# The feed-forward block of a Perceiver layer, run two groups further behind the output projection

## The chip, the cores and the metric

The kernel runs on one core of a Trainium2 chip, in one launch. The time is the device time of the program in microseconds (us). A core has TensorE (PE: matmuls and transposes, which write to PSUM), VectorE (DVE), ScalarE (ACT), GpSimd (POOL) and SyncE (SP, which here issues the DMAs). Each engine works through its own instruction list in order and waits on semaphores for the others.

## The reference

One layer of three blocks, each with a residual: cross-attention of x (32 x 32 x 256) to a context (32 x 257 x 256), causal linear attention with random features over 16 heads, and a feed-forward block with quantised inputs and ternary weights. The change touches only the end of the second block and the third:

```python
x = x + (y @ Wo)                                   # end of the linear attention
a = layernorm(x)
s = 127 / clip(max|a| over the row, 1e-5);  aq = round(a * s) / s
h = gelu(aq @ quantise(w1).T)                      # 256 -> 1024
t = 127 / clip(max|h| over the row, 1e-5);  hq = round(h * t) / t
x = x + hq @ quantise(w2).T                        # 1024 -> 256
```

Rounding is done by adding and then subtracting ROUND = 12582912; the integers are exact in bf16. The scales are per row, so each row's absmax must be known before anything of it is rounded.

## The kernel before

The 1024 rows of x are 8 groups (NG) of 128 rows, one row per partition. The first two blocks take the trace up to about 233 us and are not touched. The last stage runs over the groups; the order on each engine is written out by hand in a loop over i, in which each step works on the group `i - k` with a k of its own. For a group g the steps are, in the order in which the data passes:

- `yTt` (PE, L1079) transposes the attention's output in eight 128x128 blocks into the banks b0 and b1; `yTc` copies them to yT, half on ACT (shown at L387, the line of the helper `copy`), half on DVE (L784).
- `project_out` (PE, L1101): 16 fp32 matmuls into b2. The trace shows each as x16.
- `x2` (DVE): residual add (L796), then the statistics (L573, L576) and epsilon (L578). `rstd` (POOL, L295) takes the power -0.5.
- `quant_a` (DVE): normalises into xn3 (L583), absmax (L813) and three small operations for the scales (L802 to L805). `round_a` (POOL, L367) multiplies and adds ROUND; `cast_a` (ACT, L508) subtracts it into bf16 `aq`.
- `aqTt` (PE, L1109) transposes aq into b3, `aqTc` (ACT, helper `copy`) copies it to `aqT`. There is one aqT, so aqTc(g) waits until layer1 of group g-1 has read it (`h_mm`).
- `layer1` (PE, L1120): four bf16 matmuls 128x512 into b45, in two halves. `gelu` (ACT, L522) takes each half to `hid[g % 2]`.
- `quant_h` (DVE): absmax over 1024 columns (L818), then the scales. `round_h` (POOL, L373) writes hid times scale plus ROUND to `hr`, `cast_h` (ACT, L529) subtracts it into bf16 `hq`. hr and hq exist once each.
- `hqTt` (PE, L1129): eight transposes into b6, `hqTc` (ACT, helper `copy`) copies them to hqT.
- `layer2` (PE, L1139): eight bf16 matmuls into b7; it waits until `final` of the group before has read b7 (`fin_r`).
- `final` (DVE, L827): scales b7 and adds the residual, into `fin[g % 2]`. SP stores it.

Before the change layer1 and aqTt are one group behind project_out, gelu and quant_h two, hqTt and layer2 three, final four. When project_out of the last group is through, PE has by its list done layer1 of groups 0 to 5 and layer2 of groups 0 to 3.

Of the kernel before, what the change touches and what calls it, by code (L numbers as in the profile page):

```python
# [18 lines left out]
BF16 = mybir.dt.bfloat16  # L19
ALU = mybir.AluOpType  # L20
# [3 lines left out]
P = 128  # L24
B, T, D = 32, 32, 256
L = 257
NG = B * T // P
BG = P // T
PT = 2 * T
DC = D // P  # L30
# [5 lines left out]
HALF = NG // 2  # L36
# [5 lines left out]
ROUND = 12582912.0  # L42
# [3 lines left out]
def build(nc, x, ctx, ctxT, xWq, bq, xWk, bk, xWvT, bv, aWq, aWk, aWv, aWo, Wf, w1T, w2T,  # L46
          ident_d, mask_d, seq_d, out):
    with ExitStack() as stack:
        def sem(name):
            return stack.enter_context(nc.semaphore(name))  # L50

        def bank(name, shape, dt=F32):
            return stack.enter_context(nc.psum_tensor(name, shape, dt))
# [19 lines left out]
        w1q = keep.take("w1q", [P, DC, HID], BF16)  # L73
# [19 lines left out]
        qsc = keep.take("qsc", [P, 8, NG])  # L93
# [55 lines left out]
        z3 = Region(work_at)  # L149
# [1 line left out]
        xn3 = z3.take("xn3", [P, D])  # L151
        xr3 = z3.take("xr3", [P, D])
        aq = z3.take("aq", [P, D], BF16)
        aqT = z3.take("aqT", [P, DC, P], BF16)
        hid = [z3.take(f"hid{i}", [P, HID]) for i in range(2)]
        hr = z3.take("hr", [P, HID])
        hq = z3.take("hq", [P, HID], BF16)
# [6 lines left out]
        b0, b1, b2, b3 = (bank(f"b{i}", [P, 512]) for i in range(4))  # L164
        b45 = bank("b45", [P, 2, 512])
# [6 lines left out]
        def qk_bank(h, c):  # L172
# [41 lines left out]
        a_scale, ar_r, aq_r, aqT_mm, aqT_cp = (sem(n) for n in ("a_scale", "ar_r", "aq_r", "aqT_mm", "aqT_cp"))  # L214
        h_mm, h_act, h_scale, hr_r, hq_r, hqT_mm, hqT_cp, f2_mm, fin_r = (
            sem(n) for n in ("h_mm", "h_act", "h_scale", "hr_r", "hq_r", "hqT_mm", "hqT_cp", "f2_mm", "fin_r"))
# [60 lines left out]
        def _(pool):  # L277
# [15 lines left out]
            def rstd(n, g):  # L293
                pool.wait_ge(ln_var[n], g + 1)
                nc.gpsimd.tensor_tensor(lnr[:, n, g:g + 1], lnv[:, n, g:g + 1], mh[:, 0:1],  # L295
                                        ALU.pow).then_inc(ln_rstd[n], 1)
# [65 lines left out]
            def round_a(g):  # L362

                pool.wait_ge(a_scale, g + 1)
                if g >= 1:
                    pool.wait_ge(aq_r, g)
                nc.gpsimd.tensor_scalar(xr3[:], xn3[:], qsc[:, 2, g:g + 1], ROUND, ALU.mult, ALU.add).then_inc(ar_r, 1)  # L367

            def round_h(g):
                pool.wait_ge(h_scale, g + 1)  # L370
                if g >= 1:
                    pool.wait_ge(hq_r, g)
                nc.gpsimd.tensor_scalar(hr[:], hid[g % 2][:], qsc[:, 6, g:g + 1], ROUND, ALU.mult,  # L373
                                        ALU.add).then_inc(hr_r, 1)

            for i in range(NG + 2):
                if 0 <= i - 2 < NG:
                    round_h(i - 2)
                if i < NG:
                    rstd(2, i)  # L380
                    round_a(i)


        @block.scalar
        def _(act):
            def copy(dst, src):
                return nc.scalar.activation(dst, src, ACT.Copy)  # L387
# [121 lines left out]

            def aqTc(g):  # L510
                act.wait_ge(aqT_mm, g + 1)
                if g >= 1:
                    act.wait_ge(h_mm, 2 * g)
                copy(aqT[:], b3[:].bitcast(BF16)[:, 0:D]).then_inc(aqT_cp, 1)

            def gelu(g):
                if g >= 2:
                    act.wait_ge(hr_r, g - 1)
                act.wait_ge(out_scale[0], g + 1)
                for c in range(2):  # L520
                    act.wait_ge(h_mm, 2 * g + c + 1)
                    nc.scalar.activation(hid[g % 2][:, 512 * c:512 * c + 512], b45[:, c, :], ACT.Gelu,  # L522
                                         scale=qsc[:, 3, g:g + 1]).then_inc(h_act, 1)

            def cast_h(g):
                act.wait_ge(hr_r, g + 1)
                if g >= 1:
                    act.wait_ge(hqT_mm, g)
                nc.scalar.activation(hq[:], hr[:], ACT.Copy, bias=-ROUND).then_inc(hq_r, 1)  # L529

            def hqTc(g):
                act.wait_ge(hqT_mm, g + 1)
                if g >= 1:
                    act.wait_ge(f2_mm, g)
                copy(hqT[:], b6.bitcast(BF16)).then_inc(hqT_cp, 1)

            yTc(0)
            act.wait_ge(s_mask, STEPS)
            for i in range(NG + 4):
                if 0 <= i - 2 < NG:  # L540
                    gelu(i - 2)
                if 0 <= i - 1 < NG:
                    cast_a(i - 1)
                    aqTc(i - 1)
                if 0 <= i - 3 < NG:
                    hqTc(i - 3)
                if i + 1 < NG:
                    yTc(i + 1)
                if 0 <= i - 2 < NG:
                    cast_h(i - 2)  # L550


        @block.vector
        def _(dve):
# [261 lines left out]
            def quant_h(g):  # L816
                dve.wait_ge(h_act, 2 * g + 2)
                link(nc.vector.tensor_reduce(qsc[:, 4, g:g + 1], hid[g % 2][:], AX.X, ALU.max,  # L818
                                             apply_absolute_value=True))
                scales(4, 1, g, h_scale)  # L820

            def final(g):
                dve.wait_ge(f2_mm, g + 1)
                dve.wait_ge(out_scale[1], g + 1)
                if g >= 2:
                    dve.wait_ge(stored[g % 2], 16 * (g // 2))
                nc.vector.scalar_tensor_tensor(out=fin[g % 2][:], in0=b7[:, 0:D], scalar=qsc[:, 7, g:g + 1],  # L827
                                               in1=res[:, g, :], op0=ALU.mult, op1=ALU.add).then_inc(fin_r, 1)

            for i in range(NG + 4):  # L830
                if 0 <= i - 4 < NG:
                    final(i - 4)
                if 0 <= i - 2 < NG:
                    quant_h(i - 2)
                if i < NG:
                    x2(i)
                if i + 1 < NG:
                    yTc(i + 1)
                if i < NG:
                    quant_a(i)  # L840
# [3 lines left out]
        def _(pe):  # L844
# [8 lines left out]
            for m in range(DC):  # L853
                for c in range(DC):
                    mm = pe.matmul(b4[:, m * D:(m + 1) * D], xwq[:, c, m * P:(m + 1) * P], xwk[:, c, :],  # L855
                                   start=(c == 0), stop=(c == DC - 1))
# [7 lines left out]
            for m in range(DC):  # L864
                for c in range(DC):
                    mm = pe.matmul(b5[:, 260 + 2 * m:262 + 2 * m], xwk[:, c, m * P:(m + 1) * P],
                                   bqk[:, 0, c:c + 1].broadcast_to([P, 2]), start=(c == 0), stop=(c == DC - 1))
# [244 lines left out]
            def layer1(g):  # L1112
                pe.wait_ge(aqT_cp, g + 1)
                if g == 0:
                    pe.wait_ge(w_quant, 4)
                for hh in range(2):
                    if g >= 1:
                        pe.wait_ge(h_act, 2 * g - 1 + hh)
                    for c in range(DC):
                        mm = pe.matmul(b45[:, hh, :], aqT[:, c, :], w1q[:, c, 512 * hh:512 * (hh + 1)],  # L1120
                                       start=(c == 0), stop=(c == DC - 1))
                    mm.then_inc(h_mm, 1)

            def hqTt(g):
                pe.wait_ge(hq_r, g + 1)
                if g >= 1:
                    pe.wait_ge(hqT_cp, g)
                for c in range(HC):
                    mm = pe.transpose(b6.bitcast(BF16)[:, c * P:(c + 1) * P], hq[:, c * P:(c + 1) * P], identb[:])  # L1129
                mm.then_inc(hqT_mm, 1)  # L1130

            def layer2(g):
                pe.wait_ge(hqT_cp, g + 1)
                if g == 0:
                    pe.wait_ge(w_quant, 8)
                if g >= 1:
                    pe.wait_ge(fin_r, g)
                for c in range(HC):
                    mm = pe.matmul(b7[:, 0:D], hqT[:, c, :], w2q[:, c, :], start=(c == 0), stop=(c == HC - 1))  # L1139
                mm.then_inc(f2_mm, 1)  # L1140

            pe.wait_ge(f_exp, 8 * PAIRS)
            for i in range(NG + 4):
                if i < NG:
                    project_out(i)
                if 0 <= i - 1 < NG:
                    aqTt(i - 1)
                if 0 <= i - 3 < NG:
                    hqTt(i - 3)
                if i + 1 < NG:  # L1150
                    yTt(i + 1)
                if 0 <= i - 1 < NG:
                    layer1(i - 1)
                if 0 <= i - 3 < NG:
                    layer2(i - 3)


# [30 lines left out]
```

## Time and profile before

| | us |
|---|---|
| runs of the kernel before | 304.04, 306.99, 348.58 (median 306.99) |
| profiled execution, its own time | 302.64 |
| its span, first to last instruction | 300.1 |
| first project_out starts | 233.07 |
| last `final` | starts 297.40, takes 0.48 |
| store behind the last `final`, to landing | 1.7 |
| busy in the whole span: PE, DVE, ACT, POOL | 262.3, 169.3, 140.0, 127.4 |
| mean granted clock of PE, share of the full clock | 0.962 |

Times in the rows count from the first instruction of the span. A row of the timeline merges instructions of one line that follow each other on one engine; its time runs from the start of the first to the end of the last. A bracket at its end says how long the engine had been idle before it and what released it. In the chain of waits each piece is the time that it adds to the chain, so it can be shorter than the instructions themselves. PEld are weight loads, which run beside the matmuls.

### The profile page before, as it was taken

How to read it: one execution, taken by the hardware profiler on the slowest of the kernel's cores; microseconds unless marked ns; L12 is line 12 of the kernel's file. 1: busy time of each engine (PE TensorE's matmuls, PEld its weight loads, DVE VectorE, ACT ScalarE, POOL GpSimd, SP SyncE). 2: the span in 40 equal slices, each digit the busy share in tenths (PEclk: the TensorE clock that was granted, in tenths of full speed). 3: DMA queues.
4: the chain of work that ended last, by engine and by line, in shares of the span. 5: the costliest groups of instructions: out<-in, count | busy, mean ns of one | idle time of the engine just before them, and what ended most of it. 6: DMA issues, size and time to landing. Idle time of an engine off the chain costs nothing.

```text
span 300.1 us, 6276 instructions
## 1 busy us (share of the span) xinstructions
PE 262.3 (87%) x2438; PEld 192.0 (64%) x2442; DVE 169.3 (56%) x440; ACT 140.0 (47%) x260; POOL 127.4 (42%) x124
## 2 busy tenths in 40 slices
PE   0867848899997979999999999999989899999753
PEld 0743425566665757777777777777768777888532
DVE  4664567665543254555555555555555558777740
ACT  1032404233333775555555555555543055666662
POOL 2150044111021254558585858585894024323320
PEclk9996859999999999999999999999999999999995
DMA  7999985475019201000001010100000000000011
GB/s 231 323 369 400 351 298 151 167 282 141 3 9 367 78 8 30 20 20 16 22 2 35 4 37 2 35 2 2 2 0 2 2 1 2 17 19 20 17 35 35
DMA packets 17487, 26.70 MB, mean 89 GB/s; under 512 B 1428, under 2 KB 10804, under 8 KB 17460
## 3 DMA queue, kind: packets, MB, share of 16 engines
q1 hardware_dynamic: 17460, 26.32, 25.9%
q8 instruction: 19, 0.31, 0.4%
q14 instruction: 8, 0.07, 0.1%
HBM read 25.27 MB, written 1.05 MB: 88 GB/s over the span
## 4 chain that ended last, share of the span: by engine, by line
PE 75%; DVE 8%; ACT 5%; issue 5%; POOL 2%; DMA 2%; SPq 1%; POOLq 0%; DVEq 0%; ACTq 0%
PE b L1023 15%; PE b L847 9%; PE b L1101 8%; PE b L849 7%; PE b L848 7%; PE b L1048 6%; PE b L1036 5%; PE b L903 3%; PE b L1079 2%; PE b L926 2%; DMA bqk<-in_bk 2%; PE b L1139 2%; PE b L1120 1%; PE b L923 1%; PE b L855 1%
## 5 line engine op out<-in xcount | busy, mean ns | idle before, releaser
L490 ACT ACTIVATE phi<-b 128x512 f32<-128x512 f32 x64 | 34.8, 595 | 42.2 <-PE b L1023 42.2
L336 POOL TENSOR_TENSOR sq_lo<-sq,sq_hi 128x512 fp32r<-128x512 f32 x32 | 40.8, 1286 | 30.9 <-ACT sq_hi L448 30.1
L707 DVE CAST x_hi<-b 128x512 fp32r<-128x512 f32 x32 | 22.1, 691 | 46.7 <-ACT sq_hi L448 46.7
L295 POOL TENSOR_TENSOR lnr<-lnv,mh 128x1 f32<-128x1 f32 x16 | 8.8, 550 | 77.0 <-DVE lnv L578 77.0
L1101 PE MATMUL b<-wo,yT 128*128 128x256 f32 x128 | 29.3, 382 | 1.5 <-ACT yT L387 1.2
L847 PE MATMUL b<-nT_lo,wp_hi 128*128 128x512 f32 x64 | 27.0, 421 | 0.8 <-DVE x_lo L709 0.8
L1101 PEld LDWEIGHTS b<-wo,yT 128*128 128x128 f32 x128 | 23.7, 190 | 5.7 <-ACT yT L387 1.4
L849 PE MATMUL b<-nT_hi,wp_hi 128*128 128x512 f32 x64 | 25.4, 396 | 0.0
L848 PE MATMUL b<-nT_hi,wp_lo 128*128 128x512 f32 x64 | 25.3, 395 | 0.0
L447 ACT ACTIVATE sq<-b 128x512 f32<-128x512 f32 x32 | 19.2, 599 | 12.3 <-PE b L849 12.3
L709 DVE TENSOR_TENSOR x_lo<-b,x_hi 128x512 fp32r<-128x512 f32 x32 | 22.1, 692 | 1.1
L387 ACT ACTIVATE va<-b 128x512 f32<-128x512 f32 x16 | 9.6, 600 | 26.0 <-PE b L849 25.6
L1036 PEld LDWEIGHTS b<-phi,phi 128*64 128x64 f32 x512 | 16.2, 138 | 5.6 <-issue 5.4
L583 DVE TENSOR_SCALAR xn<-res,lnm,lnr 128x256 f32<-128x256 f32 x24 | 15.2, 642 | 6.9 <-POOL lnr L295 6.5
L448 ACT ACTIVATE sq_hi<-b 128x512 fp32r<-128x512 f32 x32 | 19.0, 594 | 0.0
L1036 PE MATMUL b<-phi,phi 128*64 128x64 f32 x512 | 18.4, 225 | 0.0
L1048 PE MATMUL b<-va,smk 64*64 64x65 f32 x512 | 18.4, 221 | 0.0
L1023 PE MATMUL b<-x_hi,feat_hi 64*128 64x512 f32 x64 | 16.9, 495 | 1.6 <-ACT phi L490 1.6
L847 PEld LDWEIGHTS b<-nT_lo,wp_hi 128*128 128x128 f32 x64 | 12.0, 187 | 8.5 <-issue 5.1
L1048 PEld LDWEIGHTS b<-va,smk 64*64 64x64 f32 x512 | 16.2, 134 | 1.6 <-issue 0.6
L847 PE MATMUL b<-wv_lo,nT_hi 128*128 128x512 f32 x32 | 13.9, 434 | 2.9 <-DVE nT_lo L682 2.9
L373 POOL TENSOR_SCALAR hr<-hid,qsc 128x1024 f32<-128x1024 f32 x8 | 9.0, 1125 | 16.8 <-DVE qsc L804 16.8
(143 smaller groups left out, 573.8 us busy)
## 6 DMA issues: line engine op xcount, KB each, us to landing
cT<-in_ctxT SPq DMA_DIRECT2D x8, 1028.0 KB, 8.6
cn<-in_ctx SPq DMA_DIRECT2D x8, 1024.0 KB, 6.8
res<-in_x SPq DMA_DIRECT2D x2, 512.0 KB, 4.1
wv_raw<-in_aWv SPq DMA_DIRECT2D x1, 1024.0 KB, 18.1
wp_raw<-in_aWq SPq DMA_DIRECT2D x8, 128.0 KB, 2.3
wp_raw<-in_aWk SPq DMA_DIRECT2D x8, 128.0 KB, 2.9
w_raw<-in_w1T SPq DMA_DIRECT2D x1, 1024.0 KB, 5.0
w_raw<-in_w2T SPq DMA_DIRECT2D x1, 1024.0 KB, 7.7
```

The costliest lines, as they stand in the source:

```text
L336: nc.gpsimd.tensor_tensor(sq_lo[s % 2][t][:], sq[s % 2][t][:], sq_hi[s % 2][t][:].bitcast(F32), ALU.subtract).then_inc(sq_l, 1)
L447: nc.scalar.activation(sq[s % 2][t][:], (b0, b1)[t][:], ACT.Square).then_inc(sq_f, 1)
L490: nc.scalar.activation(phi[s % 2][t][a][:], (b2, b3)[a][:], ACT.Exp).then_inc(f_exp, 1)
L707: nc.vector.tensor_copy(x_hi[s % 2][t][:], (b0, b1)[t][:]).then_inc(x_h, 1)
L709: nc.vector.tensor_tensor(x_lo[s % 2][t][:], (b0, b1)[t][:], x_hi[s % 2][t][:].bitcast(F32), ALU.subtract).then_inc(x_l, 1)
L847: pe.matmul(acc, l_hi, r_lo, start=first, stop=False)
L848: pe.matmul(acc, l_lo, r_hi, start=False, stop=False)
L849: return pe.matmul(acc, l_hi, r_hi, start=False, stop=last)
L1023: mm = pe.matmul((b2, b3)[a][:], w[rows, :], v[rows, :], start=(n == 0), stop=(n == 4))
L1036: mm = pe.matmul(b45[PT * b:PT * (b + 1), h, (a * HALF + g) * PT:(a * HALF + g + 1) * PT], phi[h][1][a][:, at], phi[h][0][a][:, at], start ...
L1048: mm = pe.matmul(b67[keys, a, g * VW:(g + 1) * VW], smk[h][keys, a * HALF + g, :], va[keys, HALF * h + g, pair * 2 + a, :], start=True, st ...
L1101: mm = pe.matmul(b2[:, 0:D], yT[g % 2][:, c, :], wo[:, c, :], start=(c == 0), stop=(c == HC - 1))
```

## The change

- layer1 is three groups behind project_out instead of one, gelu and quant_h four instead of two, hqTt, hqTc and layer2 five instead of three, final six instead of four. aqTt, aqTc, cast_a and all before them stay where they are.
- aqT gets a buffer per group, and aqTc waits for layer1 no more.
- round_h and cast_h of groups 4 to 7 (HALF is 4) are done by DVE, by a new function cast_h; POOL and ACT keep those of groups 0 to 3.
- In DVE's loop quant_h (and cast_h) stand ahead of final, where final stood ahead of quant_h.

```diff
-        aqT = z3.take("aqT", [P, DC, P], BF16)
+        aqT = z3.take("aqT", [P, NG, DC, P], BF16)
 # POOL
-            for i in range(NG + 2):
-                if 0 <= i - 2 < NG:
-                    round_h(i - 2)
-                if i < NG:
-                    rstd(2, i)
-                    round_a(i)
+            for i in range(NG):
+                if 0 <= i - 4 < HALF:
+                    round_h(i - 4)
+                rstd(2, i)
+                round_a(i)
 # ACT
             def aqTc(g):
                 act.wait_ge(aqT_mm, g + 1)
-                if g >= 1:
-                    act.wait_ge(h_mm, 2 * g)
-                copy(aqT[:], b3[:].bitcast(BF16)[:, 0:D]).then_inc(aqT_cp, 1)
+                copy(aqT[:, g], b3[:].bitcast(BF16)[:, 0:D]).then_inc(aqT_cp, 1)
...
-            for i in range(NG + 4):
-                if 0 <= i - 2 < NG:
-                    gelu(i - 2)
+            for i in range(NG + 6):
+                if 0 <= i - 4 < NG:
+                    gelu(i - 4)
                 if 0 <= i - 1 < NG:
                     cast_a(i - 1)
                     aqTc(i - 1)
-                if 0 <= i - 3 < NG:
-                    hqTc(i - 3)
+                if 0 <= i - 5 < NG:
+                    hqTc(i - 5)
                 if i + 1 < NG:
                     yTc(i + 1)
-                if 0 <= i - 2 < NG:
-                    cast_h(i - 2)
+                if 0 <= i - 4 < HALF:
+                    cast_h(i - 4)
 # DVE
-            for i in range(NG + 4):
+            def cast_h(g):
+                dve.wait_ge(h_scale, g + 1)
+                dve.wait_ge(hq_r, g)
+                nc.vector.tensor_scalar(hr[:], hid[g % 2][:], qsc[:, 6, g:g + 1], ROUND, ALU.mult,
+                                        ALU.add).then_inc(hr_r, 1)
+                dve.wait_ge(hr_r, g + 1)
+                dve.wait_ge(hqT_mm, g)
+                nc.vector.tensor_scalar(hq[:], hr[:], ROUND, None, ALU.subtract).then_inc(hq_r, 1)
+
+            for i in range(NG + 6):
                 if 0 <= i - 4 < NG:
-                    final(i - 4)
-                if 0 <= i - 2 < NG:
-                    quant_h(i - 2)
+                    quant_h(i - 4)
+                    if i - 4 >= HALF:
+                        cast_h(i - 4)
+                if 0 <= i - 6 < NG:
+                    final(i - 6)
                 if i < NG:
                     x2(i)
...
 # PE
-                        mm = pe.matmul(b45[:, hh, :], aqT[:, c, :], w1q[:, c, 512 * hh:512 * (hh + 1)],
+                        mm = pe.matmul(b45[:, hh, :], aqT[:, g, c, :], w1q[:, c, 512 * hh:512 * (hh + 1)],
...
-            for i in range(NG + 4):
+            for i in range(NG + 6):
                 if i < NG:
                     project_out(i)
                 if 0 <= i - 1 < NG:
                     aqTt(i - 1)
-                if 0 <= i - 3 < NG:
-                    hqTt(i - 3)
+                if 0 <= i - 5 < NG:
+                    hqTt(i - 5)
                 if i + 1 < NG:
                     yTt(i + 1)
-                if 0 <= i - 1 < NG:
-                    layer1(i - 1)
                 if 0 <= i - 3 < NG:
-                    layer2(i - 3)
+                    layer1(i - 3)
+                if 0 <= i - 5 < NG:
+                    layer2(i - 5)
```

## Rows read from the trace of the kernel before

**Rows 1.** The page, busy time and share of the span of each engine.
```profile
PE 262.3 (87%) x2438; PEld 192.0 (64%) x2442; DVE 169.3 (56%) x440; ACT 140.0 (47%) x260; POOL 127.4 (42%) x124
```

**Rows 2.** Chain of waits, one full turn of the stage: start us, us, what.
```profile
257.16 3.46 PE b L1101 x16
260.61 0.11 PE b L1109 x2
260.73 0.45 PE b L1129 x8
261.17 0.88 PE b L1079 x8
262.05 0.86 PE b L1120 x4
262.92 0.87 PE b L1139 x8
```

**Rows 3.** Timeline, project_out(1) to project_out(3): start us, us, engine, line, what.
```profile
242.55 0.42 DVE L796 TENSOR_TENSOR res<-b,res 128x256 f32<-128x256 f32 x1 [2.38 <-PE b L1101]
...
243.76 0.69 DVE L784 COPY yT<-b 128x512 f32<-128x512 f32 x1
...
244.55 3.69 PE L1101 MATMUL b<-wo,yT 128*128 128x256 f32 x16 [0.19 <-issue]
...
250.29 3.69 PE L1101 MATMUL b<-wo,yT 128*128 128x256 f32 x16 [0.19 <-issue]
```

**Rows 4.** Timeline, behind the last project_out.
```profile
280.54 0.42 DVE L796 TENSOR_TENSOR res<-b,res 128x256 f32<-128x256 f32 x1 [0.71 <-PE b L1101]
...
282.97 1.26 ACT L522 ACTIVATE hid<-b,qsc 128x512 f32<-128x512 f32 x2
```

**Rows 5.** Timeline, the last group; the row at 290.29 is layer2 of group 6.
```profile
289.36 1.22 DVE L818 TENSOR_REDUCE qsc<-hid 128x1 f32<-128x1024 f32 x1 [1.03 <-ACT hid L522]
...
290.29 1.11 PE L1139 MATMUL b<-w2q,hqT 128*128 128x256 bf16 x8 [1.45 <-ACT hqT L387]
...
291.06 1.12 POOL L373 TENSOR_SCALAR hr<-hid,qsc 128x1024 f32<-128x1024 f32 x1 [3.98 <-DVE qsc L804]
...
292.21 1.06 ACT L529 ACTIVATE hq<-hr 128x1024 bf16<-128x1024 f32 x1 [1.98 <-POOL hr L373]
...
293.32 1.03 PE L1129 MATMUL b<-identb,hq 128*128 128x128 bf16 x8 [1.92 <-ACT hq L529]
294.40 1.02 ACT L387 ACTIVATE hqT<-b 128x1024 bf16<-128x1024 bf16 x1 [1.13 <-PE b L1129]
...
295.48 1.89 PE L1139 MATMUL b<-w2q,hqT 128*128 128x256 bf16 x8 [1.12 <-ACT hqT L387]
297.40 0.48 DVE L827 SCALAR_TENSOR_TENSOR fin<-b,qsc,res 128x256 f32<-128x256 f32 x1 [5.48 <-PE b L1139]
```

**Rows 6.** Groups of instructions from 233 us on: count, busy us and mean ns, idle.
```profile
L818 DVE TENSOR_REDUCE qsc<-hid 128x1 f32<-128x1024 f32 x8 | 9.8, 1220 | 3.4 <-ACT hid L522 3.3
...
L827 DVE SCALAR_TENSOR_TENSOR fin<-b,qsc,res 128x256 f32<-128x256 f32 x8 | 3.8, 478 | 7.7 <-PE b L1139 7.7
...
L583 DVE TENSOR_SCALAR xn<-res,lnm,lnr 128x256 f32<-128x256 f32 x8 | 3.3, 408 | 1.1 <-POOL lnr L295 0.7
```

**Rows 7.** Groups of instructions of DVE, two forms of 128 columns in SBUF.
```profile
L714 DVE TENSOR_TENSOR feat_lo<-feat,feat_hi 128x128 fp32r<-128x128 f32 x1 | 0.3, 293 | 0.0
...
L713 DVE CAST feat_hi<-feat 128x128 fp32r<-128x128 f32 x1 | 0.2, 212 | 0.0
```

**Rows 8.** Windows: length, busy PE, PEld, DVE, ACT, POOL, granted clock, DMA.
```profile
288.00:290.00 2.00, 0.62 (x8) 0.45 (x8) 0.97 (x2) 2.00 (x4) 0.00 (x0) 1.00 0.19 66
290.00:292.00 2.00, 1.11 (x8) 0.70 (x8) 1.49 (x5) 0.24 (x1) 0.94 (x1) 0.79 0.00 0
292.00:294.00 2.00, 0.68 (x7) 0.68 (x8) 0.00 (x0) 1.06 (x1) 0.18 (x1) 0.50 0.19 66
```

**Rows 9.** Waits from 233 us on: who waited, for whom, sum, times, longest.
```profile
ACT aqT L387 <- PE b L1109: 14.1, 8, 2.3
```

## The prediction

> **What bounds the kernel now.** The engine table of the page [rows 1] puts TensorE (PE) first with 87% of the span. That is an average over all stages, so the next view is the chain of waits, cut to the stage that is edited. In one turn of the loop [rows 2] every piece is PE's: project_out 3.46, aqTt 0.11, hqTt 0.45, yTt 0.88, layer1 0.86, layer2 0.87, in sum 6.63 us. A full turn is PE-bound, so what other engines do there costs nothing.
>
> The timeline at the hand-over from project_out(1) to project_out(2) [rows 3] shows what bounds a turn that is not full. There is no hqTt and no layer2 yet. project_out(1) ends and DVE starts the residual add at 242.55. DVE must go through add, statistics and epsilon before its half of the yT copy, which runs from 243.76 to 244.45, and project_out starts at 244.55. From one project_out to the next it is 250.29 - 244.55 = 5.74 us. PE has only 3.46 + 0.11 + 0.88 + 0.86 = 5.31 us of work in it. The short turn is bound by DVE's order, and layer1 lies hidden in it.
>
> Behind the last project_out (its reader, the residual add, starts at 280.54 [rows 4]) comes a tail of 17.3 us, to the end of the last `final` at 297.88 [rows 5]. There the last group goes from engine to engine with nothing beside it: absmax and scales on DVE from 289.36, rounding on POOL at 291.06, cast on ACT at 292.21 (done 293.27), transposes, copy, layer2, `final`. What the last groups still need once project_out is through sets the end.
>
> **What the change does, part by part.**
>
> *The delay.* All instructions of PE stay; only their place moves. By the end of project_out(7) PE has done two layer1, two hqTt and two layer2 fewer. The layer1 that go out come from turns 1 and 2, and there they were hidden under DVE's hand-over, so they give nothing. The hqTt and layer2 go out of turns 3 and 4, which become short turns: 2 x (6.63 - 5.74) = 1.8 us. Against it: quant_h(0) now stands ahead of x2(4) on DVE, and gelu(0), with its table load, can only start behind the first half of layer1(0), at 253.98 + 0.11 + 0.88 + 0.43 = 255.4. I put 0.2 on that (0 to 1). project_out(3) ends at 250.29 + 3.69 = 253.98, (4) at 259.7, (5) at 265.65, (6) at 272.3, (7) at 278.9, which is **1.6 us earlier**.
>
> *The tail.* Now four groups (4 to 7) have gelu to `final` still before them, where it was two with gelu to go. gelu(4) has the same queue ahead of it on ACT as gelu(6) had: copy of aqT, copy of hqT, cast_h. It started 282.97 - 280.54 = 2.43 us behind the last project_out and took 1.26 [rows 4]. So quant_h(4) can start at 278.9 + 3.75 = 282.65. From there DVE does, in order and for each group, quant_h, cast_h and a `final`.
>
> *The price of cast_h on DVE* is in no row: two passes over 1024 columns in SBUF with no second tensor. On POOL and ACT they take 1.12 and 1.06 [rows 5]. Upper bound: the absmax over 1024 columns, 1.22 [rows 6]. Nearer rows: over 128 columns of SBUF the cast of feat takes 0.212 and the subtraction of two tensors 0.293 [rows 7]; the add of 256 columns takes 0.42 [rows 3]. The two-tensor form thus costs 0.16 and 1.0 ns per column, the cast about 0.4 ns per column, giving a lower bound of 0.16 + 0.40 = 0.56. The normalisation over 256 columns takes 0.408 with two per-partition scalars; `final`, with one, takes 0.478 against 0.42, so a scalar is 0.06, and 0.29 is left: 0.5 ns per column [rows 3, 6]. That row is nearest, so the rounding is 0.16 + 0.51 + 0.06 = 0.73 and the cast 0.67; ends 0.56 and 1.22 each.
>
> The Trainium skill (VectorE: DVE Perf Modes, The perf-mode tier table) says that an fp32 tensor_scalar within SBUF runs at twice the rate of a two-tensor operation; an estimate from its figures is (512 + 151) / 0.96 = 0.69 us for either pass, and 1.22 at the single rate. By the first the sum below stays as it is, by the second it is that of the second rival.
>
> *One turn of DVE in the tail*: quant_h 1.70 (289.36 to 291.06 [rows 5]), rounding 0.73, cast 0.67, `final` 0.48 [rows 6], and some 0.15 for the hand-overs: 3.73 us. PE and ACT have less per group, but they are tied to DVE: layer2(g) waits for final(g-1), and layer1(g+3) stands behind it on PE. From the end of final(3) it goes through layer2(4) 1.11, hqTt(5) 0.45, copy 1.02 and gelu(7) 1.26, about 3.9 us, so gelu(7) comes 0.1 to 0.2 late (1.26 as in [rows 4]). Four turns: 282.65 + 14.9 + 0.2 = 297.75, the end of final(5).
>
> *The end.* Only then may layer2(6) run; hqTt(7) stands behind it on PE although its input has long been there, then the copy, layer2(7), final(7). The granted clock fell from 1.00 to 0.79 and 0.50, thus from 2.4 to 1.2 GHz, once PE was busy 0.6 to 1.1 us of each 2 [rows 8], and there the eight transposes took 1.03 and layer2 1.89, against 0.45 and 1.11 before [rows 2, 5]. I take the lower clock: 1.95 + 1.0 + 1.1 + 1.95 + 0.5 = 6.5 us, so final(7) ends at 304.2. At the full clock it is 4.2 us, and 301.9.
>
> *At no cost:* the buffer of aqT per group, and the wait taken from its copy; ACT waited there for the transposes each time (14.1 us, 8 times [rows 9]), never for layer1. Eight stores stay, later but spaced as DVE's turns are; the last lands behind the last `final` as now. POOL loses four roundings; rstd(7) and round_a(7) stand behind round_h(3), which is done by then.
>
> **Sum:** 304.2 - 297.9 = +6.3 us. On the profiled execution (302.64, of which 300.1 span) that is 308.9, 2.1% more. The runs shown lie above that execution, the lowest at 304.04, the median at 306.99; I start from about 304 and put **310**.
>
> **Rivals.**
> - *The clock holds.* PE has more to do in the tail than before (four layer1 in place of two), so it may stay at 2.4 GHz to the end. For it: from 288 to 290 the clock was still 1.00 with PE busy 0.62 of 2 us [rows 8]. Against: from final(5) on it has as little as now. Price: -2.3 us, thus +4.0, 306.6 on the profiled execution. It might also fall earlier; then gelu(7) is late by one to two us more, +7.5.
> - *DVE's passes at the single rate.* 1.22 each adds about 1.05 us a turn, and gelu(7)'s lateness goes: +4.1, thus +10.4, 313.0. For it only that no row has the operation; the normalisation speaks against it.
> - *The other side: the tail keeps its length.* If the end were set by the last group's passage and not by DVE's turns, the tail would be 17.3 less 0.7 (absmax to cast 3.2 in place of 3.9 [rows 5]) and start 1.6 earlier: -2.3, 300.3. It decides at the turn: the fixed pieces are 3.75 and 6.5, so not to be slower the four turns must fit in 17.3 + 1.6 - 10.25 = 8.7, or 2.2 us each. The absmax with its scales alone is 1.70. The Trainium skill (GPSIMD Engine Reference, Engine selection) sends elementwise work on a tile to VectorE, and by that rule the move is a gain; the trace agrees on the passage of one group, but before the change POOL and ACT worked beside DVE, and here all is in one queue.
>
> **How the numbers follow.** Forecast 0.50 (+5 to +8), clock holds 0.24, single rate 0.16, other side 0.10. 2% is about what a measurement of this kernel can tell, here 6.1 us. The forecast lies on that line: two thirds of it, and the single rate, are slower by over 2% (0.49); the rest, the held clock and half of the other side are within (0.46); the other half of the other side, should PE's saving be larger than 1.6 too, is faster (0.05). The range runs from the held clock on the lowest run shown less some scatter, 305, to the single rate on a base 1 to 2 us higher, 316.
>
> **What would show it.** project_out(7) ends at about 279 (wrong if still above 280); starts of project_out 5.7 apart up to the fifth; rounding and cast near 0.7 each; absmax to absmax of groups 4 to 7 about 3.7 us apart with DVE busy nearly throughout; layer2(6) released by final(5); last `final` some 25 us behind the last project_out, where it was 17.3. The forecast is wrong if DVE stands idle between these turns, which would put the end back on PE and ACT.

## The result, and the profile after

| | before | after |
|---|---|---|
| median of the runs beside each other | 305.51 | 309.49 |
| ratio, 95% interval | | 1.0161 (1.0105 to 1.0216) |
| profiled execution, span | 302.64, 300.1 | 309.54, 307.8 |
| start of the first project_out | 233.07 | 237.31 |
| from there to the end of the last | 47.43 | 45.66 |
| from there to the end of the last `final` (the tail) | 17.38 | 22.59 |
| the whole stage | 64.81 | 68.25 |

The change makes the kernel slower by 1.0 to 2.2%. Ratios compare fast executions alone (one of 348.58 us of the kernel before is in its median and not in the ratio), so 1.0161, some 4.9 us, is more than the 4.0 us between the medians. The profiled pair lies 6.9 us apart, but only half of that is in the code that was changed: 4.24 us are there before the first project_out starts. The stage itself is 3.44 us longer. That compares two different clocks: the kernel before ran its last transposes and its last layer2 at the lower one (1.03 and 1.89 us [rows 5]), the changed kernel at the full one (0.61 and 1.05, below). At equal clock the stage would be some 4.7 us longer, which is worked out (3.44 + 0.42 + 0.84), not measured.

Timeline of the changed kernel around the fourth to the seventh project_out (start, length, engine, line, what; the lines of PE and DVE have moved: project_out is L1109, residual add L793, yT copy L781). It answers to [rows 3].

```profile
258.26 0.42 DVE L793 TENSOR_TENSOR res<-b,res 128x256 f32<-128x256 f32 x1 [2.35 <-PE b L1109]
...
259.48 0.69 DVE L781 COPY yT<-b 128x512 f32<-128x512 f32 x1
...
260.27 3.69 PE L1109 MATMUL b<-wo,yT 128*128 128x256 f32 x16 [0.19 <-issue]
...
266.01 3.69 PE L1109 MATMUL b<-wo,yT 128*128 128x256 f32 x16 [0.19 <-issue]
...
272.72 3.62 PE L1109 MATMUL b<-wo,yT 128*128 128x256 f32 x16
```

The short turn is 266.01 - 260.27 = 5.74 us, as before; the first full one is 6.71. There are now two more short turns, and that is the whole gain: 47.43 - 45.66 = 1.77 us.

The same timeline behind the last project_out; it answers to [rows 4, 5]. L815 is the absmax, L830 and L834 the new rounding and cast, L824 `final`, L1147 layer2, L1137 the transposes of hq.

```profile
283.00 0.42 DVE L793 TENSOR_TENSOR res<-b,res 128x256 f32<-128x256 f32 x1 [0.32 <-PE b L1109]
...
285.43 1.26 ACT L519 ACTIVATE hid<-b,qsc 128x512 f32<-128x512 f32 x2
...
286.72 1.22 DVE L815 TENSOR_REDUCE qsc<-hid 128x1 f32<-128x1024 f32 x1 [0.32 <-ACT hid L519]
...
290.35 1.22 DVE L815 TENSOR_REDUCE qsc<-hid 128x1 f32<-128x1024 f32 x1
...
294.11 1.22 DVE L815 TENSOR_REDUCE qsc<-hid 128x1 f32<-128x1024 f32 x1 [0.25 <-ACT hid L519]
...
297.74 1.22 DVE L815 TENSOR_REDUCE qsc<-hid 128x1 f32<-128x1024 f32 x1
...
299.38 0.75 DVE L830 TENSOR_SCALAR hr<-hid,qsc 128x1024 f32<-128x1024 f32 x1
300.16 0.69 DVE L834 TENSOR_SCALAR hq<-hr 128x1024 bf16<-128x1024 f32 x1
300.77 0.48 DVE L824 SCALAR_TENSOR_TENSOR fin<-b,qsc,res 128x256 f32<-128x256 f32 x1
...
301.40 1.03 PE L1147 MATMUL b<-w2q,hqT 128*128 128x256 bf16 x8 [2.15 <-DVE fin L824]
...
302.27 0.61 PE L1137 MATMUL b<-identb,hq 128*128 128x128 bf16 x8
...
302.92 1.02 ACT L386 ACTIVATE hqT<-b 128x1024 bf16<-128x1024 bf16 x1 [2.60 <-PE b L1137]
...
303.99 1.05 PE L1147 MATMUL b<-w2q,hqT 128*128 128x256 bf16 x8 [1.11 <-ACT hqT L386]
305.08 0.48 DVE L824 SCALAR_TENSOR_TENSOR fin<-b,qsc,res 128x256 f32<-128x256 f32 x1 [2.13 <-PE b L1147]
```

Four absmaxes (groups 4 to 7) follow each other in 3.63, 3.76 and 3.63 us. layer2(6), released by final(5), had waited 2.15 us; the transposes of group 7 go behind it although their input was there at 300.85.

Windows of the changed kernel (columns as in [rows 8]); the granted clock stays at 1.00, which is 2.4 GHz, to the last matmul:

```profile
300.00:302.00 2.00, 0.60 (x6) 0.57 (x7) 1.22 (x3) 0.31 (x1) 0.00 (x0) 1.00 0.01 4
302.00:304.00 2.00, 0.89 (x13) 0.68 (x11) 0.48 (x1) 1.02 (x1) 0.00 (x0) 1.00 0.28 94
304.00:306.00 2.00, 1.04 (x8) 0.69 (x8) 0.48 (x1) 0.00 (x0) 0.00 (x0) 1.00 0.11 37
```

### The profile page after: what moved, and what is told of

Same layout as the page of the kernel before. It is cut to its first block, busy times and chain, and to the rows that moved or that the text cites. A ratio compares the mean times of both kernels' runs of the same rounds, so it can differ in the third digit from the quotient of the medians.

```text
span 307.8 us, 6273 instructions
## 1 busy us (share of the span) xinstructions
PE 265.7 (86%) x2442; PEld 194.0 (63%) x2442; DVE 175.0 (57%) x448; ACT 136.5 (44%) x256; POOL 122.6 (40%) x120
## 3 DMA queue, kind: packets, MB, share of 16 engines
HBM read 25.27 MB, written 1.05 MB: 86 GB/s over the span
## 4 chain that ended last, share of the span: by engine, by line
PE 74%; DVE 9%; ACT 6%; issue 6%; DMA 2%; POOL 1%; SPq 1%; POOLq 0%; DVEq 0%; ACTq 0%
PE b L1031 14%; PE b L855 9%; PE b L1109 8%; PE b L857 7%; PE b L856 7%; PE b L1056 6%; PE b L1044 5%; PE b L911 3%; PE b L934 2%; PE b L1087 2%; DMA bqk<-in_bk 2%; PE b L1147 1%; ACT hid L519 1%; PE b L863 1%; DVE qsc L815 1%
## 5 line engine op out<-in xcount | busy, mean ns | idle before, releaser
L1109 PE MATMUL b<-wo,yT 128*128 128x256 f32 x128 | 29.4, 383 | 3.6 <-ACT yT L386 3.3
L1109 PEld LDWEIGHTS b<-wo,yT 128*128 128x128 f32 x128 | 23.7, 190 | 8.2 <-ACT yT L386 3.9
L1147 PE MATMUL b<-w2q,hqT 128*128 128x256 bf16 x64 | 8.3, 272 | 7.6 <-DVE fin L824 6.3
```

The lines of the kernel that those rows point to most:

```text
L1109: mm = pe.matmul(b2[:, 0:D], yT[g % 2][:, c, :], wo[:, c, :], start=(c == 0), stop=(c == HC - 1))
```

## The experiments

Executions of one kernel lie up to 2% apart (19 of the kernel before: 302.9 to 308.4), and in the two profiles of that kernel all of it lies ahead of the stage, as the last experiment shows. So the experiments are read by the stage, from the start of the first project_out to the end of the last `final`; the ratios stand beside it. Each stage is of one profile. What scatters in it is the clock in the tail: the two profiles of the kernel with groups 6 and 7 on DVE are 0.85 apart by it, so a difference of up to some 1.3 us has to be checked against the clock of the two profiles.

| kernel | first project_out starts | to the end of the last | tail | stage | ratio to before |
|---|---|---|---|---|---|
| before | 233.07 | 47.43 | 17.38 | 64.81 | |
| before, again | 237.96 | 47.44 | 17.38 | 64.82 | 0.999 (0.993 to 1.005) |
| changed | 237.31 | 45.66 | 22.59 | 68.25 | 1.016 (1.011 to 1.022) |
| delay alone | 235.85 | 45.66 | 27.55 | 73.21 | 1.017 (1.007 to 1.028) |
| `final` first | 238.19 | 45.66 | 22.30 | 67.96 | none (304.1 to 310.1 beside 304.2 to 307.9) |
| groups 4 to 7 on DVE, no delay | 236.29 | 47.77 | 16.28 | 64.05 | 0.993 (0.989 to 0.997) |
| groups 6 and 7 on DVE, no delay | 232.84 | 47.43 | 15.46 | 62.89 | 0.987 (0.980 to 0.994) |
| the same, again | 234.77 | 47.44 | 14.60 | 62.04 | 0.990 (0.986 to 0.994) |
| the same with added matmuls | 236.91 | 47.44 | 14.21 | 61.65 | 0.986 (0.980 to 0.993) |
| rounding twice | 237.18 | 45.66 | 25.74 | 71.40 | 312.8, one run |

**The delay alone.**

```diff
 # against the changed kernel: POOL and ACT keep all groups
-            for i in range(NG):
-                if 0 <= i - 4 < HALF:
+            for i in range(NG + 4):
+                if 0 <= i - 4 < NG:
                     round_h(i - 4)
...
-                if 0 <= i - 4 < HALF:
+                if 0 <= i - 4 < NG:
                     cast_h(i - 4)
 # DVE
-                    if i - 4 >= HALF:
-                        cast_h(i - 4)
```

> The changed kernel with its delays and its aqT buffers, but rounding and cast of all groups on POOL and ACT as before. Measured is the stage, from the start of the first project_out to the end of the last final: 64.8 us before, 68.3 in the changed kernel. Theory A (the delay leaves four groups behind the last project_out, each of which costs a whole turn through the single hr and hq; the move to DVE only shortens that turn): the turn goes over absmax, POOL 1.12, ACT 1.06 with gelu and the hqT copy between, about 4.5 us in place of 3.65, so the stage is 71.9 at the full clock and 73 to 74 if the clock falls, 3.5 to 5.5 longer than with the move. Rival B (the delay is a gain of 1.6 to 1.8 us by shorter turns, the loss comes from DVE's load in the tail): 63 us. Both: project_out(7) ends 45.6 behind the start of project_out(0).

Measured: 73.21. The delay alone costs 8.4 us of stage, with the clock fallen at the end in both profiles; moving the rounding to DVE wins 5.0 of it back, of which 1.3 is the clock that held in the changed kernel. So the loss is the delay, not DVE's load, and rival B falls. The ratios, 1.017 and 1.016, do not show these 5.0 us; the medians are 4.5 us apart (313.99 and 309.49), but the kernel before was slower beside the first, too (307.32 against 305.51). Timeline of this kernel, one turn of the tail (L816 absmax, L373 POOL's rounding, L527 the cast, L520 gelu):

```profile
290.36 1.22 DVE L816 TENSOR_REDUCE qsc<-hid 128x1 f32<-128x1024 f32 x1 [2.98 <-ACT hid L520]
...
292.06 1.12 POOL L373 TENSOR_SCALAR hr<-hid,qsc 128x1024 f32<-128x1024 f32 x1 [3.98 <-DVE qsc L802]
...
293.21 1.06 ACT L527 ACTIVATE hq<-hr 128x1024 bf16<-128x1024 f32 x1 [1.97 <-POOL hr L373]
294.17 1.25 ACT L520 ACTIVATE hid<-b,qsc 128x512 f32<-128x512 f32 x2
...
295.45 1.22 DVE L816 TENSOR_REDUCE qsc<-hid 128x1 f32<-128x1024 f32 x1 [2.98 <-ACT hid L520]
...
304.51 1.03 PE L1136 MATMUL b<-identb,hq 128*128 128x128 bf16 x8
...
306.66 1.89 PE L1146 MATMUL b<-w2q,hqT 128*128 128x256 bf16 x8 [1.11 <-ACT hqT L387]
```

The turn is 5.09, not the 4.5 that was expected, so the number came out right partly by luck: the expectation had four turns longer by 0.9, the profiles have three longer by 1.42, an end that is 0.6 shorter at equal clock, and the lower clock. It is a closed ring: absmax and scales, rounding, cast, and only behind the cast in ACT's list the gelu of the next group, on which DVE waits 2.98 us. The kernel before has the same ring between its last two groups: the absmax of group 7 at 289.36 [rows 5] comes 5.10 behind that of group 6. Timeline of the kernel before:

```profile
284.26 1.22 DVE L818 TENSOR_REDUCE qsc<-hid 128x1 f32<-128x1024 f32 x1
```

The price of one more group in the tail is a whole ring: the tail is 27.55 - 17.38 = 10.17 us longer, two rings. The ring is one of this order on ACT; gelu of the next group ahead of the cast was not tried.

**The move alone, groups 6 and 7, and groups 4 to 7.**

```diff
 # against the kernel before; FROM is 6 or 4; cast_h on DVE is the changed kernel's
 # POOL, ACT: round_h and cast_h
-                if 0 <= i - 2 < NG:
+                if 0 <= i - 2 < FROM:
 # DVE
                 if 0 <= i - 2 < NG:
                     quant_h(i - 2)
+                    if i - 2 >= FROM:
+                        cast_h(i - 2)
```

> The kernel before with the new cast_h on DVE for groups 6 and 7 alone; final stays ahead of quant_h and no delay is changed. Theory A: these two groups have nothing beside them in DVE's queue but final, their passage loses the hand-overs to POOL and ACT (rounding and cast 1.45 in place of 2.2 with 0.15 of hand-over), and gelu(7) no longer stands behind cast_h(6) on ACT: the stage is 61.4 at the full clock, 62.6 if the clock falls as before, so 2.2 to 3.4 us shorter than before. Rival B (DVE's load is the loss): 64.8 or more.

> The kernel before with the new cast_h on DVE for groups 4 to 7 and no delay. Groups 4 and 5 are now rounded on DVE while project_out still runs. Theory A: 62.7 at the full clock, 64 if it falls, project_out(7) ends 0.3 later since residual add and yT copy come later on DVE, so 1 to 1.5 us worse than with groups 6 and 7 alone, but not slower than before. Rival B: slower than before, 66 or more.

Measured: 62.89 and 64.05, within 0.3 of theory A's numbers for the lower clock (62.6 and 64) and against rival B; as ratios 0.987 and 0.993. The 1.9 us won by the first are a little under the 2.2 that were expected at least. The move is a gain, and a larger one for the two groups that are behind the last project_out. The clock was not the same in the two: with groups 4 to 7 it was down to 0.50 from 292 to 294 us and back at 1.00 from 296 on, so there the last transposes and layer2 took 0.62 and 1.05. With groups 4 and 5 as well, project_out(7) ends 0.34 later. Timeline of that kernel: the cast of group 4 waits for the transposes of group 3, the residual add of project_out(6), which was over at 277.10, is queued behind it, and with it the yT copy for which project_out(7) waits until 280.37.

```profile
277.76 0.69 DVE L837 TENSOR_SCALAR hq<-hr 128x1024 bf16<-128x1024 f32 x1 [0.67 <-PE b L1140]
...
278.37 0.42 DVE L796 TENSOR_TENSOR res<-b,res 128x256 f32<-128x256 f32 x1
...
279.58 0.69 DVE L784 COPY yT<-b 128x512 f32<-128x512 f32 x1
```

One turn later the cast of group 5 (284.73) holds up the residual add of the last project_out, over at 284.06, until 285.34.

**`final` first.**

```diff
 # against the changed kernel, DVE
+                if 0 <= i - 6 < NG:
+                    final(i - 6)
                 if 0 <= i - 4 < NG:
                     quant_h(i - 4)
                     if i - 4 >= HALF:
                         cast_h(i - 4)
-                if 0 <= i - 6 < NG:
-                    final(i - 6)
```

> The changed kernel with final ahead of quant_h and cast_h in DVE's loop, as it was before the change. In the changed kernel final(5) waits behind cast_h(7), and layer2(6) and the transposes of group 7 wait for final(5). Theory A (that order holds the end back): layer2(6) and hqTt(7) are through before cast_h(7) is, the stage is 66.9 in place of 68.3. Rival C (DVE's turn is a sum, in whatever order it does the pieces, and a final that comes first has to wait for its layer2): 68.3 or up to 1 us more.

Measured: 67.96, 0.3 less than in the changed kernel. But here the granted clock fell, there it did not. Timeline and windows of this kernel, a `final` with the absmax behind it, last transposes, last layer2:

```profile
294.61 0.48 DVE L824 SCALAR_TENSOR_TENSOR fin<-b,qsc,res 128x256 f32<-128x256 f32 x1
...
295.00 1.21 DVE L815 TENSOR_REDUCE qsc<-hid 128x1 f32<-128x1024 f32 x1
...
301.59 1.04 PE L1137 MATMUL b<-identb,hq 128*128 128x128 bf16 x8 [0.58 <-DVE hq L834]
...
303.75 1.89 PE L1147 MATMUL b<-w2q,hqT 128*128 128x256 bf16 x8 [1.11 <-ACT hqT L386]
```

```profile
300.00:302.00 2.00, 1.42 (x13) 1.01 (x13) 1.90 (x5) 0.00 (x0) 0.00 (x0) 0.69 0.01 4
302.00:304.00 2.00, 0.89 (x8) 0.56 (x7) 0.00 (x0) 1.02 (x1) 0.00 (x0) 0.50 0.19 66
```

At 0.61 and 1.05, as in the changed kernel, these two are 1.27 shorter, which would make the stage 66.7, near the expected 66.9. What it shows without that correction: the transposes of group 7 now wait for the cast, not for layer2(6). The order was worth some 1.5 us of the loss at equal clock; that number is worked out, not measured, and the times of the whole kernel (304.1 to 310.1) do not decide it.

**Rounding twice.**

```diff
 # against the changed kernel, DVE's cast_h
                 dve.wait_ge(hq_r, g)
+                nc.vector.tensor_scalar(y[:, 0, :], hid[g % 2][:], qsc[:, 6, g:g + 1], ROUND, ALU.mult, ALU.add)
                 nc.vector.tensor_scalar(hr[:], hid[g % 2][:], ...)
```

> The changed kernel with DVE's rounding of groups 4 to 7 done twice (the first time into y, which nobody reads any more). Theory A (the tail is DVE's turns one behind the other): each turn is 0.75 to 0.8 longer, less the 0.15 to 0.25 for which DVE waited for gelu(6), so the stage is 68.25 + 2.8 = 71.1 at the full clock. Rival E (the tail is bound by the way over final, layer2, layer1 and gelu, and DVE has room): under 69.5.

Measured: 71.40, but with a half clock on layer2(6) and the transposes behind it. Timeline:

```profile
297.08 0.75 DVE L831 TENSOR_SCALAR hr<-hid,qsc 128x1024 f32<-128x1024 f32 x1
...
298.86 1.21 DVE L815 TENSOR_REDUCE qsc<-hid 128x1 f32<-128x1024 f32 x1
...
303.18 1.87 PE L1148 MATMUL b<-w2q,hqT 128*128 128x256 bf16 x8 [2.60 <-DVE fin L824]
304.84 1.06 PE L1138 MATMUL b<-identb,hq 128*128 128x128 bf16 x8
```

With 0.84 and 0.45 taken off it would be 70.1, 1.9 above the changed kernel: between theory A (71.1) and rival E (69.5), so neither holds as put. The absmaxes are now 4.09 apart (290.69, 294.78, 298.86), an added pass takes 0.67 from start to start, and so DVE's own turn is 4.09 - 0.67 = 3.42; in the kernel with `final` first they are 3.42 apart too (291.58, 295.00, 298.43). The changed kernel's mean is (297.74 - 286.72) / 3 = 3.67. In the kernel with `final` first the absmax starts 0.39 behind the start of the `final` ahead of it (294.61, 295.00). In the changed kernel it starts 0.59, 0.73 and 0.59 behind, thus 0.20, 0.34 and 0.20 later. The last of the three, timeline of the changed kernel, its absmax above at 297.74:

```profile
297.15 0.48 DVE L824 SCALAR_TENSOR_TENSOR fin<-b,qsc,res 128x256 f32<-128x256 f32 x1
```

The difference is the other ring. This is the chain of waits of the changed kernel through its last turn:

```profile
293.38 0.49 DVE fin L824
...
294.01 1.03 PE b L1147 x8
295.04 0.46 PE b L1137 x8
...
295.52 0.47 ACT hqT L386
...
296.44 1.27 ACT hid L519 x2
297.71 0.02 issue
297.74 1.23 DVE qsc L815
```

final(3), layer2(4), transposes and copy of group 5, gelu(7), absmax(7): the absmax waits for the gelu, although DVE is busy up to 297.63. Both rings are nearly as long; the one over PE and ACT is the longer by 0.20 to 0.34 a turn.

**Added matmuls.**

```diff
 # against the kernel with groups 6 and 7 on DVE, PE's loop
+            def fill(n):
+                for _ in range(n):
+                    pe.matmul(b0[:], identb[:], w1q[:, 0, 0:512], start=True, stop=True)
...
                     hqTt(i - 3)
+                if i - 3 >= 6:
+                    fill(4)
...
                     layer2(i - 3)
+                if i - 3 == 6:
+                    fill(3)
```

The first condition holds once more behind layer2(7), so the kernel has four added matmuls more than the expectation names, 15 in all; the last four start at 297.88 and run beside the last `final`, which does not wait for them.

> The version with groups 6 and 7 rounded on DVE and no delay, with matmuls added on PE whose result nobody reads: four bf16 128x512 (0.21 us each) behind hqTt(6), three behind layer2(6), four behind hqTt(7), all in gaps in which PE waits for ACT or DVE. Theory A (the clock fell to 0.50 because PE had too little to do in the tail, and that cost 0.43 on the last transposes and 0.84 on the last layer2): the granted clock stays at 1.00, the stage is 61.6 in place of 62.9. Rival D (the clock falls whatever PE is given here): 62.9 or, as the added matmuls then take 0.43 each and overrun their gaps, up to 64.

> Groups 6 and 7 rounded on DVE, no delay, the same kernel a second time, beside the one with added matmuls. Theory A: stage 62.9 as before (61.6 if the clock should hold by itself), the start of the first project_out scatters by some us.

Measured: 61.65, with the clock at 1.00 to the end. The same kernel without them had 62.89 in one profile, with transposes and layer2 at 1.03 and 1.89, and 62.04 in the other, with 0.62 and 1.44. Timeline of the kernel with them, and its window:

```profile
295.26 0.62 PE L1140 MATMUL b<-identb,hq 128*128 128x128 bf16 x8 [0.35 <-DVE hq L837]
295.71 1.03 PE L1155 MATMUL b<-w1q,identb 128*128 128x512 bf16 x4
...
296.99 1.05 PE L1150 MATMUL b<-w2q,hqT 128*128 128x256 bf16 x8 [0.25 <-ACT hqT L387]
```

```profile
296.00:298.00 2.00, 1.75 (x13) 1.02 (x12) 0.00 (x0) 0.94 (x1) 0.00 (x0) 1.00 0.20 66
```

Of this one profile theory A's numbers are right to 0.05. But the changed kernel's clock held by itself, so one profile does not show that the matmuls did it, and in time the two versions can't be told apart (0.986 with, 0.990 without, intervals overlapping; medians 301.9 and 303.4 on one chip). Of the versions tried it has the shortest stage and the lowest median.

**The kernel before, again.** No edit.

> The kernel before, unchanged, for a second profile. Theory A on the 4.2 us by which the first project_out started later in the changed kernel (237.3 against 233.1), in code that the change does not touch: scatter of each execution through the granted clock in the first 50 us; a second profile of the kernel before starts it anywhere from 232 to 239, with a stage within 0.3 us of 64.8. Rival F (the changed program shifts it): 233.1 again within 0.5.

Measured: the first project_out starts at 237.96, 4.9 later than in the first profile of the very same kernel, and the stage is 64.82. Windows of 25 us, of the first profile and of this one (columns as above):

```profile
25.00:50.00 25.00, 19.50 (x142) 10.24 (x142) 13.79 (x42) 7.35 (x17) 4.91 (x5) 0.73 0.80 285
```

```profile
0.00:25.00 25.00, 14.48 (x60) 10.69 (x60) 13.33 (x43) 4.04 (x7) 7.61 (x13) 0.86 0.93 315
25.00:50.00 25.00, 16.98 (x118) 7.68 (x115) 12.56 (x39) 5.93 (x16) 3.59 (x3) 0.68 0.76 277
```

Up to 50 us PE got through fewer instructions at a lower clock, as in the changed kernel (0.86 and 0.66). In the first profile of the kernel before the first window was at 1.00. So 4.24 us ahead of the stage are within the scatter of one and the same kernel, and rival F falls. Over the ten profiles the start of the stage goes with the clock of the first 25 us: two had 0.99 and 1.00 there and start the first project_out at 232.8 and 233.1; the eight with 0.86 to 0.93 start it at 234.8 to 238.2. That the clock is the cause is not shown; it may fall with whatever held PE up.

## Why the prediction was right, and where not

- **The two short turns.** Forecast 1.6 us earlier (1.8 less 0.2 for quant_h(0)); measured 1.77. The sign that was given in absolute time, project_out(7) done at about 279 and wrong above 280, fails: it was done at 282.97, because the stage began 4.24 later. Counted from the first project_out it took 45.66, where the forecast has 278.9 - 233.07 = 45.8. The delay by quant_h(0) did not come: its scales were done at 264.03, the residual add started at 264.00, right at its time.
- **The start of the tail.** quant_h(4) at 3.75 behind the last project_out: 286.72 - 282.97 = 3.75.
- **The price of the passes.** Forecast 0.73 and 0.67; measured 0.75 and 0.69. The rival at the single rate falls. The Trainium skill (VectorE: DVE Perf Modes, The perf-mode tier table) has a tensor_scalar on fp32 in SBUF at twice the rate of a two-tensor operation, and 0.69 was the estimate from it; the trace agrees for the cast, and the rounding, which has a scalar per partition, took 0.06 more.
- **DVE's turn.** Forecast 3.73 and a gelu that is 0.1 to 0.2 late; measured 3.67, of which DVE's own is 3.42 and the rest is the lateness of gelu (0.20, 0.34, 0.20). The four turns took 301.25 - 286.72 = 14.5 us and not 15.1. The term that was too large is the hand-overs: 0.15 a turn was added for them, and DVE starts its next instruction up to 0.1 before the last one's end (`final` takes 0.48, the absmax starts 0.39 behind its start). So DVE's queue, which the forecast took as the bound of a turn, is not quite it: the forecast named idle time of DVE between the turns as a sign of being wrong, and there is some, 0.11, 0.25 and 0.11 us. A turn is bound by the way over PE and ACT, and that costs 0.7 us in all over DVE's own turns.
- **The end** is where it failed: the step that took the lower clock for the last three steps of PE. In the changed kernel's profile the clock held, and from final(5) to the end it took 305.56 - 301.25 = 4.3 us and not 6.5 (4.2 was the figure at the full clock). That was a rival, with 0.24; it is what the profile shows. The forecast also compared 1.03 for the transposes with 0.45, a piece of the chain; their time at the full clock is 0.61. The forecast of +6.3 for the stage is thus +3.4: 2.2 from the clock, 0.6 from the turns, 0.2 from the start. In all three other profiles with four groups in the tail (delay alone, `final` first, rounding twice) the clock did fall, so it could not be read off the kernel before.
- **The base.** I started from 304 where the kernel before has its median at 305.5 to 307.3; its profiled execution was one of the fastest. Too low a base and too high an increase made 310 come out beside 309.49. The number was good partly by luck; the sign and the tail's share rest on the steps above.
- **The other side** (the tail keeps its length) falls: 22.6 in place of 17.4. Its test was right: four turns had to fit in 2.2 us each, and took 3.67. The rule of the Trainium skill (GPSIMD Engine Reference, Engine selection) that elementwise work on a tile goes to VectorE agrees with the move alone, which took 0.8 us (groups 4 to 7) and 1.9 and 2.8 us (groups 6 and 7) off the stage; it was not what decided.

What stays open: why the stage starts up to 4.9 us later in some executions, what kept the clock up in the changed kernel's tail, and whether the added matmuls are what kept it up in the last version.

## What to carry to other kernels

Work that a bound engine does under a long phase can be taken out of it by running it later, but it comes back behind the phase, where nothing covers it: here two groups of delay won 1.8 us and, with rounding left where it was, cost 10.2 in the tail. Count the groups that are still to go when the long phase ends, and multiply by the ring that one of them needs (absmax, rounding, cast, next gelu: 5.1 us over four hand-overs, 3.4 to 3.7 with rounding on DVE). Shorten the ring of the last groups only, on the engine that is idle by then, and leave the depth alone: that version is 1.0 to 1.3% faster than the kernel before (two measurements, with intervals from 0.6 to 2.0%).

## What had not been expected of the hardware

The granted clock in the first 50 us differs between executions of one kernel (1.00 and 0.73 in its two windows, or 0.86 and 0.68), and with the lower one all that follows came 4.9 us later; whether the clock is the cause is open. In the tail it fell in some executions and held in others at much the same busy time of PE: it held in the changed kernel with 0.60 of 2 us and was down to 0.50 in the kernel before after 0.62 and 1.11 [rows 8]. In the kernel with groups 4 to 7 on DVE it fell to 0.50 (292 to 294 us) and came back to 1.00 (from 296 us on) within the tail.
